# Products of keys and values made early, a third pair of banks, and products of zeros on TensorE where it waits

## The reference, cut to what matters

```python
x = x + _L0_xattn_ref(_layernorm(x), ctx, ...)   # 16 heads of 16, inputs and weights rounded to int8 steps
x = x + _L0_ffn_ref(_layernorm(x), ...)          # mixture: 2 of 8 experts (F = 176) and a shared expert
x = x + _L1_xattn_ref(_layernorm(x), ctx, ...)   # "wide": 16 heads of 128
x = x + _L1_ffn_ref(_layernorm(x), ...)          # low-rank experts
x = x + _L2_xattn_ref(_layernorm(x), ctx, ...)   # retention
x = x + _L2_ffn_ref(_layernorm(x), ...)          # mixture: 2 of 8 experts (F = 704), no shared expert
x = x + _L3_xattn_ref(_layernorm(x), ctx, ...)   # attention over features
x = x + _L3_ffn_ref(_layernorm(x), ...)          # MLP of 1024 and 8 of 512 single-row experts per token
```

```python
q = (inputs_q @ Wq).reshape(b, sq, H, HD) * (1.0 / np.sqrt(HD))
k = (inputs_kv @ Wk).reshape(b, skv, H, HD)
v = (inputs_kv @ Wv).reshape(b, skv, H, HD)
attn = jax.nn.softmax(jnp.einsum('bqhd,bkhd->bhqk', q, k), axis=-1)
return jnp.einsum('bhqk,bkhd->bqhd', attn, v).reshape(b, sq, H * HD) @ Wo
```

```python
ew = jax.nn.silu(jnp.einsum('nh,nkh->nk', x, down_embed[indices])) * jax.nn.softmax(scores, axis=-1)
experts_states = jnp.einsum('nk,nkh->nh', ew, up_embed[indices])
mlp = jax.nn.silu(x @ gate_w) * (x @ up_w) @ down_w
```

## Time and profile before

| what | value |
|---|---|
| three runs, us | 1331.17, 1333.31, 1334.44 (median 1333.31) |
| profiled execution, us | 1332.05 |
| its span, first to last instruction, us | 1330.2 |
| mean granted clock of PE | 0.909 |
| busy, us | PE 1086.9, DVE 622.7, ACT 365.7, POOL 224.2 |
| chain that ended last | PE 70%, DVE 18%, issue 4%, ACT 3%, DMA 3% |

### The profile page before, as it was taken

One profiled execution on the slowest core, in us unless ns is written; L12 is line 12 of the kernel. 1 busy time (PEld: TensorE's weight loads), 2 busy tenths in 40 slices (PEclk: granted clock), 3 DMA queues, 4 the chain that ended last, 5 costly groups with the idle time before them and its releaser, 6 DMA issues.

```text
span 1330.2 us, 17690 instructions
## 1 busy us (share of the span) xinstructions
PE 1086.9 (82%) x6754; PEld 758.2 (57%) x6754; DVE 622.7 (47%) x1459; ACT 365.7 (27%) x666; POOL 224.2 (17%) x301
## 2 busy tenths in 40 slices
PE   5869895398998889965675499999819999969988
PEld 4655684166667666654564467777605555533466
DVE  6967222434343343357545512222146677438454
ACT  4632121122221222211110112222102444425653
POOL 4313332400000000001111111110071222011232
PEclk9977998599999999998886699999957999979998
DMA  9001132101010010064001511211050000010000
GB/s 264 4 1 64 44 90 78 36 24 33 4 33 33 28 33 4 33 232 159 0 1 44 201 29 33 80 33 28 21 180 15 2 1 1 1 64 0 0 12 20
DMA packets 36954, 65.31 MB, mean 49 GB/s; under 512 B 4456, under 2 KB 27848, under 8 KB 35464
## 3 DMA queue, kind: packets, MB, share of 16 engines
q1 hardware_dynamic: 26504, 47.91, 10.7%
q0 software_dynamic: 3744, 10.23, 2.9%
q10 hardware_dynamic: 6624, 6.03, 1.3%
HBM read 53.93 MB, written 10.22 MB: 48 GB/s over the span
## 4 chain that ended last, share of the span: by engine, by line
PE 70%; DVE 18%; issue 4%; ACT 3%; DMA 3%; POOL 2%; SPq 0%; DVEq 0%; ACTq 0%
PE bank L344 22%; PE bank L1132 11%; PE bank L1156 6%; PE bank L1923 5%; PE bank L1378 4%; PE bank L1386 2%; PE bank L1967 2%; PE bank L1946 2%; PE bank L1938 2%; PE bank L1145 1%; DVE big L1243 1%; PE bank L1363 1%; PE bank L1356 1%; PE bank L1978 1%; PE bank L2371 1%
## 5 line engine op out<-in xcount | busy, mean ns | idle before, releaser
L1132 PE MATMUL bank<-big 128*128 x552 | 153.7, 422 | 3.7 <-ACT big L1006 2.4
L344 PE MATMUL bank<-XNT,big 128*128 128x512 f32 x296 | 140.1, 622 | 14.8 <-issue 9.6
L1132 PEld LDWEIGHTS bank<-big 128*128 128x128 f32 x552 | 96.5, 191 | 50.4 <-issue 11.8
L265 POOL TENSOR_TENSOR rstd<-ve,half 128x1 f32<-128x1 f32 x64 | 38.7, 604 | 494.3 <-DVE ve L259 494.2
L1923 PE MATMUL bank<-big,xs 32*128 32x512 f32 x256 | 85.7, 718 | 37.4 <-DVE xs L271 33.6
L1831 DVE TENSOR_REDUCE big<-bank 128x2 f32<-128x512 f32 x128 | 82.2, 685 | 49.3 <-PE bank L1923 49.2
L344 PEld LDWEIGHTS bank<-XNT,big 128*128 128x128 f32 x296 | 56.4, 198 | 80.3 <-issue 70.7
L1156 PE MATMUL bank<-big 128*128 (+1 forms) x368 | 87.2, 380 | 1.1 <-ACT big L1021 1.1
L1883 ACT ACTIVATE big<-bank 128x1024 f32<-128x1024 f32 x64 | 62.0, 1021 | 67.7 <-PE bank L1946 67.7
L950 DVE TENSOR_TENSOR big<-big,bank 128x704 f32<-128x704 f32 x23 | 20.5, 889 | 124.6 <-ACT big L1014 124.6
L344 PE MATMUL bank<-CTXT,big 128*128 128x512 f32 (+1 forms) x192 | 67.0, 494 | 10.8 <-DMA big<-wvT 10.8
(11 more groups left out here) (340 smaller groups left out, 1878.6 us busy)
## 6 DMA issues: line engine op xcount, KB each, us to landing
big<-m_gu SPq DMA_DIRECT2D x8, 1408.0 KB
big<-a_qkv SPq DMA_DIRECT2D x16, 384.0 KB, 3.9
big<-m_d SPq DMA_DIRECT2D x8, 768.0 KB
yg<-big ACTq DMA_DIRECT2D x46, 128.0 KB, 1.7
big<-m_gu SPq DMA_DIRECT2D x8, 352.0 KB
big<-a_o SPq DMA_DIRECT2D x16, 128.0 KB, 2.4
big<-p_gu SPq DMA_DIRECT2D x1, 2048.0 KB, 7.7
big<-m_d SPq DMA_DIRECT2D x8, 176.0 KB
```

Source lines behind the costliest of these rows:

```text
L265: e.tensor_tensor(k.rstd[p][:, :], k.ve[p][:, :], k.half[:, :], ALU.pow).then_inc(k.ln_rstd, 1)
L344: ins = e.matmul(out, a, b, start=start and n == 0, stop=stop and n == len(pairs) - 1)
L1132: ins = e.matmul(out, xgT[s % 2][:, kb, :], WB[:, bass.ds(at[s] + (kb * 2 * F + c * chunk), chunk)], start=kb == 0, stop=kb == KB - 1)
```

## The change

One helper is new, and is called at five places: 6 products at the start of `attention_qdq`, 8, 7 and 3 in the mixture without shared expert, 3 at the start of `peer_mlp`. The banks that it writes hold nothing at that time.

`attention_wide`: keys and values of heads 0 to 3 are made by `pe_first` and copied by `act_first`, which the engines run ahead of the wait for X; they go in turn through the bank pairs 2, 4 and 6. The weights `w3`, `kT` and `v` have four buffers. `project(h)` makes only queries for these heads. SP loads four heads at the start and then head h + 4 when head h is done with its buffer. The normalising takes one tile at a time with the statistics two ahead, where it took pairs.

`peer_mlp`: gate products use three bank pairs, `MINE` is 4, all `embed` products come ahead of the first `down`, and the order of the expert weights on PE, DVE and ACT changes.

```diff
+def keep_busy(e, k, b, n):
+    for _ in range(n):
+        e.matmul(k.bank[:, b, :], k.zeros[:, :], bc(k.zeros[:, :], 1, 4), start=True, stop=True)
...
@@ attention_qdq, pe
+        keep_busy(e, k, 6, 6)
         e.wait_ge(S["wk_ld"], 48)
...
@@ experts, pe
+        if not shared_expert:
+            keep_busy(e, k, 7, 8)
         after(e, "mk", 1)
...
+        if not shared_expert:
+            keep_busy(e, k, 7, 7)
         for q in (0, 1):
             after(e, "hot", q + 1)
...
             after(e, "shy", NT)
+        else:
+            keep_busy(e, k, 4, 3)
         after(e, "wts", ends["wts"])
...
@@ attention_wide, sp
+        for h in range(FIRST):
+            load(h)
+        load_o(0)
+        load_o(1)
+        for h in range(H):
+            if h + FIRST < H:
+                if h < FIRST:
+                    e.wait_ge(S["qk_ps"], qk_at(h + 1))
+                else:
+                    e.wait_ge(S["v_ps"], h - FIRST + 1)
+                load(h + FIRST)
+            if 1 <= h < H - 1:
+                e.wait_ge(S["wo_ps"], 4 * h)
+                load_o(h + 1)
...
@@ attention_wide, act and pe
+    def act_first(e):
+        for h in range(FIRST):
+            e.wait_ge(S["f_ps"], 2 * h + 1)
+            e.copy(v[h], k.bank[:, first_bank(2 * h):first_bank(2 * h) + 2, :].rearrange("p b (t d) -> p (b t) d", d=HD))\
+                .then_inc(S["f_sb"], 1)
+            e.wait_ge(S["f_ps"], 2 * h + 2)
+            e.copy(kT[h], k.bank[:, first_bank(2 * h + 1):first_bank(2 * h + 1) + 2, :].rearrange("p b n -> p (b n)"))\
+                .then_inc(S["f_sb"], 1)
+    def first_bank(n):
+        return 2 + 2 * (n % 3)
+    def pe_first(e):
+        for h in range(FIRST):
+            e.wait_ge(wsem[h], 16)
+            for n in (2 * h, 2 * h + 1):
+                if n >= 3:
+                    e.wait_ge(S["f_sb"], n - 2)
+                b = first_bank(n)
+                if n % 2 == 0:
+                    ins = values(e, h, b)
+                else:
+                    for c in (0, 1):
+                        ins = mm(e, k.bank[:, b + c, :], [(w3[h][:, 1, kb], k.CTXT[:, kb, c * HALF:(c + 1) * HALF])
+                                                         for kb in range(KB)])
+                ins.then_inc(S["f_ps"], 1)
...
+        def project(h):
+            e.wait_ge(wsem[h % FIRST], 16 * (h // FIRST + 1))
+            for n in range(2 if h < FIRST else 4):
...
+            if h >= FIRST:
+                values(e, h, VB).then_inc(S["v_ps"], 1)
...
@@ peer_mlp
-    MINE = 5
+    MINE, SETS = 4, (0, 2, 6)
...
-            if n >= 2:
-                e.wait_ge(S["h"], n - 1)
+            if n == 2:
+                e.wait_ge(S["r_sb"], 2)
+            if n >= 3:
+                e.wait_ge(S["h"], n - 2)
...
+        keep_busy(e, k, 0, 3)
         for t in range(4):
             turn(t)
...
         for n in range(IB):
             gate_up(IB + n)
-            if n in (2, 4, 6):
-                turn_w(n // 2 - 1)
-        for u in range(UB):
-            down(u)
-            if u == 0:
-                turn_w(3)
-            down_e(u)
-            embed(EB + u)
-            if u in (1, 2):
-                turn_w(3 + u)
-        for u in range(UB, NT):
+            if n % 2 == 1:
+                turn_w(n // 2)
+        for n in range(EB):
+            embed(EB + n)
+            if n == 2:
+                turn_w(4)
+        for u in range(NT):
             down(u)
             down_e(u)
-            if u < UB + 2:
-                turn_w(u + 2)
+            if u in (0, 2, 3):
+                turn_w(5 + (u + 1) // 2)
...
@@ program, run
             for n, s in enumerate(stages):
+                if who + "_first" in s:
+                    s[who + "_first"](e)
                 if n > 1 and who != "sp":
                     e.wait_ge(k.x_tile, LOADED + 8 * (n - 1))
```

More of the change, by code:

```diff
@@ L1183, in attention_wide @@
     HALF = T // 2
+    FIRST = 4
     at0, done0 = 8 * l, LOADED + 8 * l
     A = Arena(k.arena_buf, 16200)
-    W = Arena(k.late, 8800)
-    w3 = [W.take(3, KB, HD) for _ in (0, 1)]
+    W, W2 = Arena(k.late, 2048), Arena(k.late[:, 6900:8800], 1900)
+    w3 = [a.take(3, KB, HD) for a in (W, W, W2, W2)]
     wo = [W.take(D) for _ in (0, 1)]
     qT = [A.take(T) for _ in (0, 1)]
-    kT = [A.take(T) for _ in (0, 1)]
-    v = [A.take(NT, HD) for _ in (0, 1)]
     s_sb = A.take(NT, SEQ)
@@ L1266, in pT_copy @@
                 .then_inc(S["pt_dve"], 1)
[L1268 to L1278, removed]
+        for h in range(H):
+            softmax(h)
+            if h + 1 < H:
+                v_copy(h + 1)
+            pT_copy(h)
+            if h > 0:
+                e.wait_ge(S["wo_sb"], 4 * (h - 1) + 2)
                 out_add(h - 1)
[L1280 to L1283, removed]
         e.wait_ge(S["wo_sb"], 4 * (H - 1) + 2)
@@ L1316, in act @@
         e.sem_inc(S["qk_sb"], 2)
[L1317 to L1328 removed]
+        qk_copy(0)
+        for h in range(H):
+            exp(h)
+            if h + 1 < H:
+                qk_copy(h + 1)
+            rest(h)
@@ new lines, in first_bank, with values @@
+    def first_bank(n):
+        return 2 + 2 * (n % 3)
+    def values(e, h, b):
+        for t in range(NT):
+            ins = mm(e, k.bank[:, b + t // 4, (t % 4) * HD:(t % 4 + 1) * HD],
+                     [(k.CTXT[:, kb, t * P:(t + 1) * P], w3[h % FIRST][:, 2, kb]) for kb in range(KB)])
+        return ins
+    def pe_first(e):
[12 more added lines that the diff above has]
+                ins.then_inc(S["f_ps"], 1)
@@ L1365, in turn_p, with out_proj @@
             ins.then_inc(S["pt_ps"], 1)
-        def out_proj(h, p, half, last=False):
-            e.wait_ge(osem[p], half * 16 + 16)
+        def out_proj(h, last=False):
+            e.wait_ge(osem[h % 2], 16 * (h // 2 + 1))
             e.wait_ge(S["c_sb"], h + 1)
@@ L2039, in peer_mlp @@
     eT = A.take(2, EB, HALF)
-    sg = [A.take(HALF) for _ in (0, 1)]
+    sg = [A.take(HALF) for _ in SETS]
     away = [W.take(NE) for _ in (0, 1)]
@@ L2191, in dve @@
         product(IB + 1)
+        weighted(0)
         hot_sum(1)
         product(IB + 2)
-        weighted(0)
         hot(2)
         product(IB + 3)
+        weighted(1)
+        hot_sum(2)
         product(IB + 4)
-        hot_sum(2)
-        weighted(1)
+        hot(3)
         product(IB + 5)
-        hot(3)
+        weighted(2)
+        hot_sum(3)
         product(IB + 6)
-        hot_sum(3)
+        hot(4)
         product(IB + 7)
-        weighted(2)
-        hot(4)
+        hot_sum(4)
         weighted(3)
-        hot_sum(4)
+        hot(5)
+        hot_sum(5)
+        weighted(4)
+        hot(6)
         add(0)
-        hot(5)
-        add(1)
-        hot_sum(5)
-        add(2)
-        hot(6)
-        add(3)
-        weighted(4)
         hot_sum(6)
         weighted(5)
+        add(1)
         hot(7)
-        add(4)
+        hot_sum(7)
+        add(2)
         weighted(6)
-        hot_sum(7)
-        add(5)
+        add(3)
         weighted(7)
-        add(6)
-        add(7)
+        for u in range(4, NT):
+            add(u)
     def act(e):
```

228 lines of the change are left out of this document (93 added, 135 removed).

## The result

The changed kernel takes 1290.89 us (median of four, 1282.84 to 1291.57) against 1333.3: a ratio of 0.967, 95% interval 0.963 to 0.971. The forecast was 1277 with a range of 1268 to 1300. The profiled execution spans 1289.4 us, where that of before spans 1330.2, so 40.8 went, and 13.9 that the forecast had are missing in the median.

The account below looks back on a forecast made before the run. The prediction took the chain on PE (TensorE) and its clock to bound most of the span. Its terms, -3.0 -40.0 -0.9 -3.0 -9.1 = -56.0, brought 1333.31 us to 1277, range 1268 to 1300.

Parts of the forecast that it names:

- First loads: First stage: zeros raise the clock so the first tile's keys, queries and values run faster; -3.0, bounds -3.2 and +2.3.
- attention_wide: Early keys and values, tile-wise normalising, and no waits before projections: -40.0 in all, bounds -27 and -43.
- C: attention_wide: waits at each second head are PE's instruction fetch, not weights; 9.6 stay, 1287; chance given as B and C 0.12.
- E: attention_wide: the early products wait behind X after all; 1297; chance 0.04.
- D: attention_wide: PE without its 28 us rest is throttled and runs at low clock; above 1500 with all sixteen heads; chance 0.04.
- B: attention_wide's gain is short: clock falls in heads 0 to 2, or ScalarE's queue holds softmax; 1290; B and C 0.12.
- Second mixture's front: Zeros ahead of counts, lists and first gather: counts later, lists and gate products faster; -0.9, bounds -2.5 and +15.
- Last stage's front: Three products of zeros let the first gate product run at full clock; -3.0, bounds -3.0 and +1.
- Tail: Last stage's second half: fewer waits for expert weights and less low clock, 3 us of stalls staying; -9.1, bounds -3 and -12.
- Rival A: All places with zeros: products of zeros do not raise the clock; 25 us more, 1302; chance 0.14.
- The sum: Whole kernel: the five terms add to -56.0, from 1333.31 to 1277, with PE's sum of other work unchanged.

Follow-up runs that it names:

- the repeated one: The changed kernel run and profiled once more with nothing altered: 1290.62 us, ratio 0.9652.
- fill: The changed kernel with 32 products of zeros in TensorE's idle time before feature attention: 1291.82 us, ratio 0.968.
- between: Five zeros ahead of the counts, the filled gap, and a product of zeros behind each of feature attention's first 20 score products: 1320.04 us, ratio 0.9886.
- attention alone: The kernel before with the new attention_wide and its early hook, no zeros, last stage as before: 1299.62 us, ratio 0.9724.
- no zeros: The changed kernel without any product of zeros, all else the same: 1290.49 us, ratio 0.9665.
- two copies: The changed kernel with two copies in DVE's queue ahead of feature attention: 1290.38 us; also tried with five zeros ahead of the counts: 1286.05 us.
- six copies: The changed kernel with five zeros ahead of the counts and six copies in DVE's queue ahead of feature attention: 1284.92 us, ratio 0.965.
- zeros alone: The kernel before with only the five keep_busy calls added: 1340.83 us, ratio 1.0045.
- fifth tile: The changed kernel with the fifth tile's weights turned after the first down product: 1290.76 us, ratio 0.9681.
- five zeros: The changed kernel with five products of zeros instead of eight ahead of the counting products: 1278.41 us, ratio 0.9586.
- the buffers alone: The changed kernel with four sets of weights, keys and values, but no keys or values made early: 1313.76 us, ratio 0.9853.

## Why the prediction was right in part

- **First loads**, -3.0: the maxima are 2.6 earlier, the stage is 3.0 shorter in this profile and 2.7 in the repeated one. Zeros and keys as forecast, low start included; DVE's normalising takes back 0.6. In two of the eleven traces with these zeros (fill, between) the stage took 96.6 and 96.9, with a low stretch of 3.4 us in its first 30, so -1.3 can happen too.
- **attention_wide**, -40.0: -40.4 and -40.0 in the two profiles of the change, -38.9 to -40.1 in four other kernels with the same stage, and -35.3 to -37.7 in five (attention alone, no zeros, two copies, six copies, zeros between). In these five PE stands 2.8 to 3.4 us in its early products, in gaps of up to 1.2 with no releaser shown (no zeros: `PE bank L350 <- issue: 3.3, 5, 0.8`), and in four of them, all but attention alone, a low stretch begins there (241 to 244 us); the others have neither. What PE waits for in them was not tried, so -40.0 is the better of two outcomes, and the forecast has no term for the other. The early work alone is worth 29.7 (forecast 29.4), the buffers with the normalising by tiles 10.7 (forecast 9.6 + 1). Starts of heads 0 to 3 9.7, 12.2, 12.2 apart (9.6, 12.2, 12.2). Rivals C and E are refuted by the waits and the window, D by a full clock. Of B nothing is left in heads 0 to 2 (weighting products 1.95 to 2.02); the first projection starts low (4.94, where the next ones take 3.70), 1.2 of the 1.6 to 3.3 that the forecast allowed.
- **Second mixture's front**, -0.9: counts 3.5 late (3.2), lists -1.8 (-2.0), expert products after them -1.7 (-1.6), in all -0.6 in this profile and -1.1 in the repeated one. The step is right and shows its fault: the eight products were three too many, worth 2.6.
- **Last stage's front**, -3.0: first gate product 6.72 to 3.67, and that it came out to the tenth is luck. Without zeros it was 5.11 and 5.15 in two kernels, so half of the gain is where a low stretch lay in the kernel before. And with zeros the clock held over the transposes behind them in seven of eleven traces (3.67) and fell in four (5.37: the repeated run, zeros alone, fill, fifth tile), among them the same program. From the end of the stage before to the products of the routing scores it is 20.0 before, 18.3 in both kernels without zeros, 16.9 to 17.1 with zeros where the clock held and 18.8 where it fell. So these three products win 1.2 or lose 0.5. What the prediction set against its own term, a clock that is low again after transposes, is what four traces show.
- **Tail**, -9.1: the stretch of 93.2 is 88.3 in the profile of after (-4.9) and 85.7 in the nine other traces with this order (-7.5), none of which has a low stretch in it; the fifth tile's run has 85.4. In two traces with the old order, attention alone and zeros alone, it is 94.8, so against those the order is worth 9.1. The terms that were off: 4.9 us of stalls for the 3.0 I allowed (the turning of tiles 2 to 4 waits 0.92, 0.61 and 2.64, the first down product 0.69; at the longest of these waits DVE's sum is late beside GpSimd's), and, in this one profile, 2.6 of low clock that I had counted as gone.
- **Rival A** is wrong as a mechanism: zeros do raise the clock (keys 1.16, counts and lists full). Yet its outcome, zeros that cost more than they bring, is what the eight and their companions do alone: 5.7 slower than before, where A would make it 18.
- **The sum.** I took every stage without an edit as unchanged in time. That step, not written down as one, failed, by +2.5, +3.3 and +5.2 in the profiled pair. For the largest, in feature attention, the traces show what differs: the same products begin at the low clock, and it rises 3 or 15 us later, and 1.6 us of delay is enough to change which. What makes it the one or the other at a given instant is not shown. Where the low stretches of the first mixture, LoRA and retention come from was not tried apart; the same program gives 132.7 and 136.1 there. That the kernel with five zeros takes 1278.41, near 1277, does not confirm the forecast: it is another kernel.

The best version is that with five products of zeros: 1278.41, 1% below the change.

## What to carry to other kernels

Waits and work that a trace shows on the bound engine can be priced place by place and added: here the early work came to 29.7 for 29.4. Where the clock changes level cannot be read from one trace: an edit anywhere ahead can cost or give 7 us in a stage that nobody touched, and even the unchanged program, profiled again, had its low stretches in other places. So take a second profile of the same program before you give a low stretch a cause or a price, and judge such an edit by the stage tables of several executions. Size filler work by the wait that it must end in, on the short side: three products too many ahead of the counts held up a whole front.

## What was not expected of the hardware

- One program's executions fall into two groups some 10 us apart: 1280.5 to 1284.8 and 1290.6 to 1291.6 in the changed kernel, at mean clocks of 0.924 to 0.927 and 0.915 to 0.921; 1307.4 and 1307.8, 1319.7 and 1321.6 with the buffers alone, at 0.922 to 0.924 and 0.906 to 0.913.
- With score products of 32 rows the clock fell 0.3 us after the first of them, behind 27.6 us of wide zeros and 1.9 of idle, and in another kernel it stayed low over 57.9 us with PE busy throughout, even with a product of zeros on all 128 rows behind each.
- Over some 3 us of transposes behind wide zeros the clock held in seven traces and fell in four, once each way in one and the same program.
- Zeros count as work for the clock: it was 1.00 over 27.6 us of nothing but zeros.
- DVE's sum over 1024 columns takes 1.23 alone and 3.10 when it starts beside a GpSimd sum of the same form, and it ends 1.1 after that one, as if it had waited for it:
```profile
1231.89 2.36 POOL L2125 TENSOR_TENSOR big<-big 128x1024 f32<-128x1024 f32 x1 [3.87 <-ACT big L2298]
1232.23 3.10 DVE L2194 TENSOR_TENSOR big<-big 128x1024 f32<-128x1024 f32 x1
```
